# Attention and mixture-of-experts layer: the row list of the first eight units made first, and one expert's low halves moved between the splits of two blocks

## The reference

```python
def _moe_forward(x, router_w, router_b, w1, b1, w2, b2, top_k=2):
    logits = jnp.einsum('bsd,de->bse', x, router_w) + router_b
    top_vals, top_idx = jax.lax.top_k(logits, top_k)
    keep = jax.nn.one_hot(top_idx, E, dtype=logits.dtype).sum(-2) > 0
    gating = jax.nn.softmax(jnp.where(keep, logits, NEG_INF), axis=-1)
    h = jax.nn.relu(jnp.einsum('td,edh->eth', xf, w1) + b1[:, None, :])
    y = jnp.einsum('eth,ehd->etd', h, w2) + b2[:, None, :]
    return jnp.einsum('etd,te->td', y, gf).reshape(B, S, D)

x = L0_attn_x
xn = _layernorm(x, axis=-1)
s = _L0_attn_ref(xn, Wq, bq, Wkv, bkv, Wo)
g = _silu(_moe_forward(xn, router_w, router_b, w1, b1, w2, b2, top_k=2))
x = x + s * g
```

## Time and profile before

| | |
|---|---|
| time, median of 3 runs | 1081.95 us (1077.45 to 1082.16) |
| span of the profiled execution | 1078.8 us; its own time is not given apart from the span |
| TensorE matmul busy | 990.9 us, 92% of the span |
| VectorE busy | 857.8 us, 80% |
| ScalarE busy | 641.9 us, 59% |
| GpSimd busy | 336.8 us, 31% |
| DMA | 172.58 MB moved, mean 160 GB/s |

### The profile page before, as it was taken

How to read it: one execution, slowest core, us unless ns; L and a number is a source line. 1 busy time by engine, 2 the same in 40 slices (tenths; PEclk the granted TensorE clock), 3 DMA queues, 4 the chain that set the end, 5 groups by cost and what they waited for, 6 DMA issues and landing times.

```text
span 1078.8 us, 25081 instructions
## 1 busy us (share of the span) xinstructions
PE 990.9 (92%) x8686; PEld 778.5 (72%) x8686; DVE 857.8 (80%) x1535; ACT 641.9 (59%) x1358; POOL 336.8 (31%) x350
## 2 busy tenths in 40 slices
PE   0747999999999999998989889999999999999997
PEld 0536888888888898865656667767777677677776
DVE  6985776666766455569999999998999999999971
ACT  2722333233333333357888888878888878788860
POOL 3215999989995000020101002121212111112111
PEclk9968999999999999999999999999999999999999
DMA  8778666666666322149887879798999878888992
GB/s 273 211 287 182 157 181 177 174 179 184 171 172 147 95 60 65 46 121 159 171 154 141 157 142 186 152 164 150 172 189 178 150 150 162 153 171 160 181 179 95
DMA packets 410137, 172.58 MB, mean 160 GB/s; under 512 B 351994, under 2 KB 399940, under 8 KB 409252
## 3 DMA queue, kind: packets, MB, share of 16 engines
q1 hardware_dynamic: 352816, 129.80, 57.5%
q10 hardware_dynamic: 50724, 23.50, 8.6%
q0 software_dynamic: 6480, 17.70, 6.5%
HBM read 52.84 MB, written 31.72 MB: 78 GB/s over the span
## 4 chain that ended last, share of the span: by engine, by line
PE 37%; DVE 10%; DMA 5%; ACT 2%; issue 1%; SPq 0%; ACTq 0%; DVEq 0%
PE b_psO L1265 11%; PE b_psS L1242 11%; PE b_psJ L1281 5%; DMA b_pT<-b_ph 5%; PE b_psJ L1201 5%; DVE b_nmax L1426 3%; DVE b_ph L1462 3%; PE b_psS L1292 2%; PE b_psO L1267 1%; PE b_psS L1201 1%; DVE b_outs L1468 1%; ACT b_pr L1346 1%; ACT b_ph L1376 1%; PE b_psS L1245 1%; DVE b_Q L1449 1%
## 5 line engine op out<-in xcount | busy, mean ns | idle before, releaser
L933 PE MATMUL psU<-bxT,w_p 128*128 128x256 f16 (+1 forms) x1920 | 287.5, 262 | 13.3 <-DVE w_p L276 9.3
L1008 ACT ACTIVATE h<-psU,bias 128x256 f32<-128x256 f32 (+1 forms) x320 | 125.3, 448 | 273.6 <-PE psU L933 171.5
L942 PE MATMUL psY<-w_p,hp 128*128 x1704 | 273.4, 273 | 2.1 <-DVE hp L1034 2.1
L1242 PE MATMUL b_psS<-b_kp,b_Q 128*128 128x512 f16 (+3 forms) x1152 | 218.8, 326 | 1.5 <-PEq L1086 1.5
L1346 ACT ACTIVATE b_pr<-b_psS,b_nmax 128x1024 f32<-128x1024 f32 (+7 forms) x256 | 187.0, 735 | 47.9 <-DVE b_nmax L1426 27.1
L933 PEld LDWEIGHTS psU<-bxT,w_p 128*128 x1920 | 188.4, 98 | 34.0 <-issue 15.1
L1265 PE MATMUL b_psO<-b_pT,b_vp 128*128 128x256 f16 x1536 | 189.7, 274 | 20.3 <-issue 13.5
L1462 DVE SCALAR_TENSOR_TENSOR b_ph<-b_pr,b_rrec,b_ph 128x1024 f16<-128x1024 f32 (+7 forms) x256 | 199.4, 810 | 0.0
L1376 ACT ACTIVATE b_ph<-b_pr,b_rrec 128x1024 f16<-128x1024 f32 (+7 forms) x256 | 187.0, 768 | 15.4 <-DVE b_rrec L1455 14.1
L1032 DVE CAST hp<-h 128x512 f16<-128x512 f32 (+1 forms) x160 | 88.9, 556 | 133.7 <-ACT h L1008 127.5
L1426 DVE TENSOR_REDUCE b_nmax<-b_psS 128x1 f32<-128x1024 f32 (+7 forms) x256 | 183.1, 746 | 13.9 <-PE b_psS L1245 12.4
(11 more groups left out here) (187 smaller groups left out, 1027.1 us busy)
## 6 DMA issues: line engine op xcount, KB each, us to landing
wstage<-in_L_ffn_w SPq DMA_DIRECT2D x48, 256.0 KB
expert_rows<-rowx SPq DMA_DIRECT2D x67, 128.0 KB
expert_outputs<-y ACTq DMA_DIRECT2D x31, 256.0 KB
a_x_all<-in_L_attn_x SPq DMA_DIRECT2D x8, 512.0 KB, 9.7
a_w_raw<-in_L_ffn_w SPq DMA_DIRECT2D x4, 1024.0 KB, 9.4
xn_split<-a_xp SPq DMA_DIRECT2D x4, 1024.0 KB, 8.9
xn_turned<-a_xT SPq DMA_DIRECT2D x3, 1024.0 KB, 13.7
b_x_row<-in_L_attn_x SPq DMA_DIRECT2D x24, 128.0 KB, 2.5
```

The lines of the kernel that those rows point to most:

```text
L933: mm = eng.matmul(psU[w % U][:, g % 2, 0:tiles * P].rearrange("p (t r) -> p t r", t=tiles), weight(n, a * W1 + c * H + g * P, P), bxT[n % ...
L942: mm = eng.matmul(psY[n % 2][:, t, :], hp[n % 2][:, a, g, t * P:(t + 1) * P], weight(n, 2 * W1 + (2 * g + b) * D, D), start=(g == 0 and k ...
L1008: a = eng.activation(h32[w % 4][:, g, 0:rows], psU[w % U][:, g, 0:rows], ACT.Relu, bias=bias[:, ds(e * HT + 2 * q + g, 1)], scale=1.0 / WS)
L1242: mm = eng.matmul(dst, Q[n % 3][:, a, u * P:(u + 1) * P], kb[:, c, lo:lo + w], start=(kk == 0), stop=(kk == 2 and not last))
```

## The change

`one_hots` made both one-hots of a chunk and all 71 columns of `who` came out together. Now the columns of the first eight units (`SOON` = `AHEAD` = 8) are made in a pass of their own. `soon_hots` writes one small one-hot for all 64 columns at once, `oh_s` (8 x 64 elements), and multiplies it by the token numbers in two halves; `lane_hots` writes the eight `oh_r`; `place_soon` adds up with 64 matmuls of 128 x 8 in another PSUM bank. Then come `owners`, the copy of 8 columns of `who`, the eight low halves of expert 0, and only then the unit one-hots of all chunks with the 64 matmuls of 128 x 71 as before, which use the same `oh_r`, and the copy of the other 63 columns. `who_` therefore counts to 2: the gathers of units 8 to 11 and the `b2b` load wait for the second count. The eight low halves of expert 1 stand between the splits of blocks 0 and 1, one behind each.

```diff
+        def place_soon(s):
+            eng.wait_ge(s_soon, s + 2)
+            for j in range(PER):
+                mm = eng.matmul(psX[:, 0:SOON], oh_r[:, s, :, j], oh_s[:, :, s * PER + j],
+                                start=(s == 0 and j == 0), stop=(s == CHUNKS - 1 and j == PER - 1))
+            if s == CHUNKS - 1:
+                mm.then_inc(s_sq, 1)
...
         project(3)
+        for s in range(CHUNKS):
+            place_soon(s)
         for s in range(CHUNKS):
             place(s)
...
+        def soon_hots():
+            cols = unit16[:, 0:SOON, 0:1].to_broadcast([P, SOON, COLS])
+            link(eng.tensor_tensor(oh_s[:, :, :], cols, q16[:, :].unsqueeze(1).to_broadcast([P, SOON, COLS]), ALU.is_equal))
+            for i in range(2):
+                half = slice(i * NT, (i + 1) * NT)
+                a = eng.tensor_tensor(oh_s[:, :, half], oh_s[:, :, half], ids16[:, :].unsqueeze(1).to_broadcast([P, SOON, NT]), ALU.mult)
+            a.then_inc(s_soon, 1)
+        def lane_hots(s):
+            at = slice(s * PER, (s + 1) * PER)
+            eng.tensor_tensor(oh_r[:, s], lane16[:, :, :], r16[:, at].unsqueeze(1).to_broadcast([P, P, PER]), ALU.is_equal).then_inc(s_soon, 1)
...
         eng.wait_ge(s_tab, 4)
+        soon_hots()
+        for s in range(CHUNKS):
+            lane_hots(s)
+        owners()
+        eng.wait_ge(s_sq, 1)
+        eng.tensor_scalar(who[:, 0:SOON], psX[:, 0:SOON], float(T * 2), None, ALU.add).then_inc(v["who_"], 1)
+        for q in range(PIECES):
+            v["first_low"](eng, q)
         for s in range(CHUNKS):
             one_hots(s)
         eng.wait_ge(s_sp, 1)
-        eng.tensor_scalar(who[:, :], psJ[:, 0:UNITS], float(T * 2), None, ALU.add).then_inc(v["who_"], 1)
-        owners()
-        for q in range(PIECES):
-            v["first_low"](eng, q)
+        eng.tensor_scalar(who[:, SOON:], psJ[:, SOON:UNITS], float(T * 2), None, ALU.add).then_inc(v["who_"], 1)
...
+        eng.wait_ge(v["who_"], 2)
         eng.dma_start(b2b[:, :], b2.rearrange("e d -> (e d)").partition_broadcast(P)).then_inc(b_l, 16)
...
-        for q in range(PIECES, FIRST):
-            v["first_low"](eng, q)
         eng.wait_ge(v["own_"], 1)
         for n in range(NBLK):
             for q in range(PAIR):
                 if q == 1 and n >= 2:
                     rows(n - 2)
                 split(n, q)
+                if n < 2:
+                    v["first_low"](eng, PIECES + PAIR * n + q)
...
-        for n in range(4, AHEAD + 4):
+        for n in range(4, AHEAD):
+            v["gather"](eng, n)
+        eng.wait_ge(v["who_"], 2)
+        for n in range(AHEAD, AHEAD + 4):
             v["gather"](eng, n)
```

More of the change, by code:

```diff
@@ L375, in routing @@
     oh_q = sb("oh_q", [P, CHUNKS, UNITS, PER], F16)
+    SOON = v["AHEAD"]
     L, L2, slot = (sb(s, [P, NT, E], F32) for s in ("L", "L2", "slot"))
+    oh_s = Arena(v["nc"], area.at - 2 * NT * E * 4).take("a_oh_s", [P, SOON, COLS], F16)
     both, oh = (sb(s, [P, 2, NT, E], F32) for s in ("both", "oh"))
@@ L425, in routing @@
         "xn", "xn_hi", "xn_lo", "turned", "out_by_act", "out_by_dve", "casts", "tables_cast"))
+    s_soon, s_sq = sem("first_one_hots"), sem("first_slots_placed")
     (s_b, s_bz, s_rh, s_rl, s_lg, s_ch, s_pos, s_diff, s_pick, s_tot, s_t16, s_cnt, s_e, s_oh, s_sp) = map(sem, (
@@ L749, in owners @@
             eng.tensor_scalar(blk_e[:, :], bf[:, 0, :], float(E - 1), None, ALU.min).then_inc(v["own_"], 1)
+        def soon_hots():
[8 more added lines that the diff above has]
+            eng.tensor_tensor(oh_r[:, s], lane16[:, :, :], r16[:, at].unsqueeze(1).to_broadcast([P, P, PER]), ALU.is_equal).then_inc(s_soon, 1)
         def one_hots(s):
             at = slice(s * PER, (s + 1) * PER)
-            step(eng.tensor_tensor(oh_r[:, s], lane16[:, :, :], r16[:, at].unsqueeze(1).to_broadcast([P, P, PER]), ALU.is_equal))
             link(eng.tensor_tensor(oh_q[:, s], unit16[:, :, :], q16[:, at].unsqueeze(1).to_broadcast([P, UNITS, PER]),
```

## The result

| | before | changed |
|---|---|---|
| time, median of six runs | 1077.59 us (1075.86 to 1082.16) | 1087.48 us (1084.86 to 1088.33) |
| ratio, 95% interval | | 1.0084 [1.0057, 1.0112] |
| span of the profiled execution | 1078.8 us | 1086.2 us |

The change makes the kernel slower: by 9.9 us between the medians, by 9.1 us by the ratio. The forecast was 1080.5 us, a change of -0.2 us, with a range up to 1085; the measured median lies outside it.

What follows compares the result with a forecast made beforehand. TensorE, full from 112 to 270 us, was taken as the bound, with GpSimd's pieces close behind; 3.0 us gained upstream were given back at block 18's wait: -0.2 us, 1080.5 us, range 1076 to 1085.

Steps and rivals of the forecast that it cites:

- TensorE 3.0 us ahead by 112: Blocks 0 to 2: block 0 starts 0.3 us earlier and 2.7 us of TensorE's idle goes.
- Blocks 7 and 9: Experts' stage: their weight pieces, near 137 and 171 plus 3.6, come before TensorE needs them at 156 and 177.
- Their term: Large place matmuls ahead of block 0: 0.12 us each, 7.6 to 7.8 for eight chunks, ending at 84.7.
- The small compare: VectorE's 512-element compare at the start of the row list: 0.6 us, with 0.4 and 0.7 as ends.
- the rival that they cost 0.12: Small matmuls of the row list at 0.12 us each: block 0 at 86.2, change +1.2, 1081.7 us; chance 5%.
- the rival that GpSimd isn't the bound: Experts' stage: nothing comes late and the 3.0 us gained upstream arrive, 1077.5 us; chance 12%.
- The rival on the clock before block 0: Unbroken placing matmuls lift TensorE's clock early: block 0 at 83.6, change -3.2, at most -6 us; chance 13%.
- the one on the 56th piece: Block 18: expert 6's last piece ends at 274.1; TensorE, there at 271.4, waits about 2.8 us and starts at 274.2.
- its terms, 105.9 and 108.2: End of the sixteenth low half, which releases gather 12: 105.9 without the late relu in block 1, 108.2 with it.
- the slack of 3.9 us: Block 18: the 56th piece ends at 270.48 in the kernel before, and TensorE needs it at 274.4.
- the slower rival: GpSimd starts later than 107.3: +3.4 us, and +1.5 for half clock at block 18; 1084 to 1086 us; chance 20%.
- its threshold of 107.4: Gather 12: from 103.47 + 3.9 on, each us of the sixteenth low half's delay is one of the kernel.

Runs made afterwards that it cites:

- the fewer early gathers: Changed kernel with every fourth of the first 32 gathers that stand between pieces made behind the last piece, with SyncE's stores: 1077.77 us, ratio 1.0001.
- the low halves alone: Kernel before with only expert 1's eight low halves moved, one behind each split of blocks 0 and 1: 1086.43 us, ratio 1.0079.
- the first form of the own semaphore: Changed kernel with expert 1's low halves counted on their own semaphore, which TensorE awaits ahead of block 2: 1087.07 us, ratio 1.0077.
- before, again: The kernel before, unchanged, run and profiled once more: 1077.54 us, ratio 0.9993.
- the 58 matmuls: Changed kernel with 58 useless 128 x 256 matmuls ahead of block 18's wait: 1080.56 us, ratio 1.002; repeated, 1084.52 us, 1.0025.

## Why the prediction was wrong

**Right, with their sizes.** The first gather was to be at 72.2 (71.86), `b2b` near 87.5 (87.70), block 0 at 84.8, or 84.5 to 85 (85.31, so a little later), TensorE 3.0 us ahead by 112 (blocks 3 to 17: 3.0 to 3.2). That last size is right partly by luck: of its two terms block 0 was 0.2 later instead of 0.3 earlier, and all 3.35 us of idle between 94 and 112 went instead of 2.7. Blocks 7 and 9 don't wait. Block 0 gains nothing since the large `place` matmuls take the place of the old wait. Their term was a little low: 7.6 to 7.8 us, or 0.12 for a matmul, and 8.73 measured, a start every 0.134. The small compare was taken at 0.6 and measured 0.69, as the rule in the Trainium skill ("VectorE: DVE Perf Modes") would have it for a step of zero; the two multiplications took 0.49, where I had 0.65, so the sum of the three was 1.18 against 1.25. That decided nothing. The small matmuls started 0.06 us apart within a chunk, as the sum had it; the rival that they cost 0.12 is refuted. So is the rival that GpSimd isn't the bound, by the wait at block 18.

**The rival on the clock before block 0** is refuted by the window 77 to 85: TensorE busy 8.00 of 8.00 us, clock 0.50. The rule that I set beside it, that sustained matmul activity lifts the clock (the Trainium skill, "TensorE: Matmul & The Clock Gate", part 1), isn't borne out by these 8 us of 128 x 71 matmuls; the clock rose at 90.6, in block 0. That is 2.4 us later than in the first profile of the kernel before (88.2), but in the second it rose at 90.3, so the difference isn't the change's.

**The step that failed** is the one on the 56th piece, "270.5 + 3.6 = 274.1 ... waits there about 2.8 us". The mechanism is right: the sixteenth low half holds GpSimd, GpSimd never makes it good, TensorE waits at block 18 with L265 as the releaser, and the wait takes back what was gained upstream. Three of its sizes were off.

1. *The start.* I took 3.6 us for gather 12; it was 4.1 (107.58 against 103.47). That is within the 2.5 to 4.8 given (its terms, 105.9 and 108.2, give 2.4 to 4.7).
2. *The stretch from gather 12 to the 56th piece (40 pieces, of which my window held 39), and the slack of 3.9 us.* This was the large one. I took both from one execution as if they were properties of the kernel. The stretch of the changed kernel was 3.2 us longer (170.2 against 167.0), with no edit in it. Start and stretch make the 56th piece 277.8, 3.7 us later than forecast, and the wait 6.3 instead of 2.8. With 172.0, as the kernel before has it too, the slack is below zero from the outset (103.47 + 172.0 = 275.5 against 274.4), and then every microsecond of gather 12's delay is one of the kernel.
3. *The clock's fall.* I put 1.5 us for it into the slower rival alone. It belonged to the sum with the wait itself: I knew of a wait of 2.8 us and let it end at full clock. It cost 1.9 us (12.35 against 10.48).

With the measured stretch and the fall in it, my sum would have been -0.2 + 3.2 + 1.9 + 0.5 = +5.4 us at block 19, against the measured 5.3. The third rival ("GpSimd starts later than 107.3", then +3.4 and +1.5, 1084 to 1086) has the right mechanism and nearly the right place, with its start at 107.58 and not at 110.8; with 20% I had it too low, because its threshold of 107.4 hung on the same slack.

The number 1080.5 came nearer to the result than the forecast change did. It stood on a base of 1078.6 to 1081.7 us, from three runs and one span, and the median of six runs is 1077.59. What was forecast was -0.2 us, and the medians differ by +9.9.

**What stays open.** Of these 9.9 us the sum above explains 5.3. From block 19 on the difference between the two profiles is 5.3, then 4.0 us at the first exponential and 7.4 at the end: attention took 607.8 and 607.9 us in both profiles of the changed kernel, and 604.5 and 603.4 before. It took 606.7 with the fewer early gathers, where no loss is left, and 601.5 to 607.9 over all profiles. Sorted by the row list, though, the four profiles with that of before have 603.4 to 604.9, and of the ten with the new one nine have 605.2 to 607.9 and one 601.5. So the new row list may cost some 2 us in attention, which would also be why kernels that start block 18 by 2.3 to 4.6 us earlier than before end only up to 3.4 us earlier, and in the medians gain 1.5 us at most. Why it should isn't known, one profile speaks against it, and no run here tests it. Putting the large `place` matmuls behind block 0, the one edit that would let block 0 use its early rows, wasn't tried, since the relu's buffer `h32` shares its memory with these one-hots.

## What to carry to other kernels

An engine that is nearly always busy and starts on a signal has its slack where its last product is used, a hundred and more microseconds on, so the cost of moving its start signal is read there. Read that slack from several executions: one of 3.9 us is none when the stretch ahead of it varies by 5.0 in one kernel. When an edit brings a new wait of several microseconds to TensorE, put the slow clock behind it into the same sum as the wait (1.9 us behind 6.31 here); and give a semaphore that counts two unlike things (here, weights for TensorE and leave for GpSimd) a second one before work is moved behind it.

## What the runs showed of the hardware

- TensorE stayed at half clock through 8 us without a gap (busy 8.00 of 8.00, matmuls of 128 x 71), and rose in block 0's matmuls of 128 x 256, at 90.6 us.
- A wait of 6.31 us brought half clock from 274.9 us for 6.8 us. In the low halves alone it was a wait of 5.56 us, and the same 6.8 us; in the first form of the own semaphore one of 8.66 us, and 10.2 us. A wait of 0.93 us (before, again) brought none, and neither did the late weights when the 58 matmuls filled the time.
- VectorE and GpSimd lengthen each other's instructions when they overlap: VectorE's cast 0.42 to 0.83 us in the rows above, its subtraction 0.69 to 1.52, a low half 0.68 to 1.47; GpSimd's subtraction 1.15 to 1.48. The Trainium skill ("SBUF — State Buffer", "SBUF: two separate sides") has a rule for it: the two share a pair of ports, which the one that starts first holds for its whole instruction. The rows agree in kind; that it is these ports isn't shown by a run here. By this rule GpSimd's pace wasn't to be taken as fixed, which the prediction did.
- The mean granted clock of an execution goes with its time. Of 111 executions of the kernel before that stood beside the experiments, the 34 with a mean of at least 0.984 have a median of 1076.5 us, the 37 with at most 0.981 one of 1082.3. Which of the two causes the other isn't shown.
